# Nine tiles of 512 and eight of 256 in place of the last twenty expert tiles of 384, with casts and hand-overs moved

## The reference

```python
y = einsum('bln,mn->blm', states, C).real + x3d @ D_mat.T
x = layernorm(x + x3d + sigmoid(res_logit) * (gelu_tanh(y @ W1) @ W2))
...
probs = softmax(xf @ Wg); weights, indices = top_k(probs, 2)
for e in range(8):
    h = gelu(xf @ W1[e] + b1[e], approximate=False)     # 128 -> 512
    y = h @ W2[e] + b2[e]                               # 512 -> 128
    out = out + y * cw[:, e:e + 1]                      # weight 0 if e was not picked
x = layernorm(x + out)
```

## Time and profile before

| | us |
|---|---|
| median of 3 runs | 317.7 (317.27 to 318.15) |
| profiled execution: its own time | 319.06 |
| profiled execution: span | 317.3 |
| PE busy in the span | 275.1 (87%) |
| DVE, ACT, POOL busy | 226.2, 211.5, 211.8 |
| first `xt` (tile 0) on PE | 115.95 |
| `xt` of tile 9, begin of the last phase | 176.21 |
| last indirect DMA of POOL starts | 283.97 |

### The profile page before, as it was taken

The page is one execution under the profiler, slowest core; times in us unless marked ns, Lnnn a source line. Parts: engine busy times, 40 slices in busy tenths (PEclk is TensorE's granted clock), DMA queues, the critical chain, the costliest instruction groups (busy, mean ns, idle before and its releaser), DMA issues.

```text
span 317.3 us, 5295 instructions
## 1 busy us (share of the span) xinstructions
PE 275.1 (87%) x1303; PEld 214.6 (68%) x1303; DVE 226.2 (71%) x721; ACT 211.5 (67%) x462; POOL 211.8 (67%) x246
## 2 busy tenths in 40 slices
PE   7789996999999939859889899999999999994910
PEld 5445563756755618758777899999999999941400
DVE  2986399757997666937766688888888989701770
ACT  3653633534745544968787799999999999910580
POOL 4375795178687878607777787778778777670680
PEclk9999998799999976979999999999999999996875
DMA  5995110121221244448888765655655654317761
GB/s 90 303 331 154 34 34 0 33 75 44 84 67 44 84 167 164 156 147 290 298 295 302 259 212 171 219 209 166 229 189 186 213 192 171 116 46 293 284 173 50
DMA packets 35687, 52.18 MB, mean 164 GB/s; under 512 B 5320, under 2 KB 26320, under 8 KB 35656
## 3 DMA queue, kind: packets, MB, share of 16 engines
q1 hardware_dynamic: 29940, 41.74, 39.6%
q0 software_dynamic: 4832, 9.97, 9.5%
q10 hardware_dynamic: 884, 0.12, 0.2%
HBM read 16.99 MB, written 13.86 MB: 97 GB/s over the span
## 4 chain that ended last, share of the span: by engine, by line
PE 39%; POOL 23%; issue 13%; SPq 8%; DVE 7%; DMA 6%; ACT 1%; ACTq 0%; POOLq 0%; DVEq 0%
POOL slots_d L479 15%; PE bank L1097 10%; PE bank L1099 9%; PE bank L1098 9%; PE bank L1184 2%; POOL rstd L469 2%; SPq L364 2%; PE bank L1201 2%; DVE work L734 2%; DMA late<-slots_d 2%; PE bank L1245 2%; PE bank L1152 2%; POOL results_d L485 2%; DMA rows<-results_d 1%; POOL early L513 1%
## 5 line engine op out<-in xcount | busy, mean ns | idle before, releaser
L485 POOL DMA_INDIRECT results_d<-work,dest x87 | 92.6, 1065 | 28.0 <-issue 25.6
L479 POOL DMA_INDIRECT slots_d<-rows,slot_i x64 | 65.6, 1025 | 28.6 <-issue 18.6
L982 DVE TENSOR_TENSOR h_l<-h,h_h 128x384 fp32r<-128x384 f32 x116 | 65.0, 561 | 18.7 <-ACT h_h L636 16.0
L631 ACT ACTIVATE h<-bank,buse 128x384 f32<-128x384 f32 x116 | 67.9, 585 | 7.2 <-PE bank L1099 3.6
L1097 PE MATMUL bank<-h_h,wuse 128*128 128x384 f32 x116 | 44.8, 387 | 3.1 <-DVE h_l L982 2.7
L1097 PE MATMUL bank<-xbt_h,wuse 128*128 128x384 f32 x116 | 41.0, 353 | 1.7 <-DVE xbt_l L968 1.3
L1099 PE MATMUL bank<-xbt_h,wuse 128*128 128x384 f32 x116 | 40.0, 345 | 0.0
L1098 PE MATMUL bank<-xbt_l,wuse 128*128 128x384 f32 x116 | 40.0, 345 | 0.0
L1099 PE MATMUL bank<-h_h,wuse 128*128 128x384 f32 x116 | 39.3, 339 | 0.0
L1098 PE MATMUL bank<-h_l,wuse 128*128 128x384 f32 x116 | 39.2, 338 | 0.0
L560 ACT ACTIVATE h<-bank 128x512 f32<-128x512 f32 x32 | 18.9, 598 | 25.0 <-PE bank L1099 24.4
(11 more groups left out here) (200 smaller groups left out, 553.0 us busy)
## 6 DMA issues: line engine op xcount, KB each, us to landing
wuse<-fw SPq DMA_DIRECT2D x37, 512.0 KB, 3.5
late<-slots_d SPq DMA_DIRECT2D x29, 195.0 KB, 2.7
fw<-in_L_ffn_W_dram SPq DMA_DIRECT2D x16, 256.0 KB, 6.1
work<-in_L_attn_x3d_dram SPq DMA_DIRECT2D x8, 256.0 KB, 6.1
rows<-results_d SPq DMA_DIRECT2D x4, 512.0 KB, 5.2
work<-results_d SPq DMA_DIRECT2D x4, 512.0 KB, 9.2
out_dram<-fw SPq DMA_DIRECT2D x8, 256.0 KB, 2.3
slots_d<-zeros SPq DMA_DIRECT2D x9, 195.0 KB, 6.4
```

The lines of the kernel that those rows point to most:

```text
L479: pool.indirect_dma_start(out=slots_d, out_offset=bass.IndirectOffsetOnAxis(ap=slot_i[:, k, i:i + 1], axis=0), in_=rows[:, k, i, :], in_of ...
L485: pool.indirect_dma_start(out=results_d, out_offset=bass.IndirectOffsetOnAxis(ap=dest[:, SQ * g + q:SQ * g + q + 1], axis=0), in_=yo[:, g ...
L631: act.activation(h32[:, b % 2, 0:SLOTS], H_PS[b % 2][:, 0:SLOTS], ACT.Gelu, bias=buse[:, k, b:b + 1]).then_inc(sm["gelu_b"], 1)
L982: dve.tensor_tensor(ht_l[b], h32[:, b % 2, 0:SLOTS], ht_h[b].bitcast(F32), ALU.subtract).then_inc(sm["hbl_ready"], 1)
```

## The change

**Tiles.** Tiles 0 to 8 stay. The twenty tiles of 384 behind them become seventeen: 512, 512, then 256 and 512 in turn, and a 256 at the end (nine of 512, eight of 256). The slots of that phase fall from 7680 to 6656, the 128-row blocks of all phases (`NCOL`) from 87 to 79. Their table needs other arithmetic on DVE (`unit_counts`, `unit_origins`, `full_tables`, `odd_tables`, in the steps of tiles 2 to 4). The result ring `yo` has 60 blocks with a place written out for each tile (`home`).

**Casts.** ACT makes all 16 weight casts; POOL keeps the subtractions, with `norm(0)` behind ten of them.

**Hand-over.** First-layer weights of tiles 0 and 1 are copied by SP, all others by DVE. SP's queue between chunks and tiles is written anew; ACT's two row copies (L537) become DMAs of SP. The routing weights of the last group, the table of tiles 3 to 8 and the first-layer weights of tile 3 move on DVE to the end of tile 1. `rows_of(7)` with the last exp and two table loads moves on ACT from tiles 1 and 2 to the head of tile 1's step, and one table load ahead of `rows_of(6)`. On PE `xt(3)` moves from the end of tile 1's step into that of tile 2.

```diff
-CASTS_BY_ACT = (3, 4, 4)
+FIRST_BY_SP = 2
+CASTS_BY_ACT = (3, 8, 5)
...
+    units = (pairs[-1] - sure[-2] * SLOTS + E * (HALF - 1)) // HALF
+    fulls = (units - E) // 2
+    LAST = fulls + E
+    MT = sure[-2] + LAST
...
+    parts = [SQ] * begins[-1] + [FQ_MAX] + [FQ_MAX, HALF // P] * E
...
+            sp.wait_ge(sm["fw_lo"], NFW)
+            sp.wait_ge(sm["route_ready"], 1)
+            first_weights(0)
+            second_weights(0)
+            for g in range(2):
+                sp.wait_ge(dispatched[g], 16 * 2 * tokens_of(g)[1])
+            load(0, 0)
+            sp.wait_ge(sm["pre_a"], HB * NCH)
+            first_weights(1)
+            load(1, 1)
+            second_rows(NCH - 2)
+            second_weights(1)
+            load(2, 0)
+            second_rows(NCH - 1)
+            for n in range(1, PHASES):
+                second_weights(begins[n] - 1)
...
                 for g in range(begins[n], ends[n]):
                     load(g, g % 2)
-                    if g == 2:
-                        sp.wait_ge(sm["pre_a"], HB * NCH)
                     if g not in begins:
                         second_weights(g - 1)
-                    if g in FIRST_BY_SP:
-                        first_weights(g)
...
             for n in range(NFW):
-                if n in (7, 13):
-                    norm((7, 13).index(n))
+                if n == 10:
+                    norm(0)
                 weights_low(n)
+            norm(1)
             norm(2)
             for g in range(NG - 1):
-                at = (5, 4, 4)[g]
+                at = (4, 4, 5)[g]
...
+            def last_softmax():
+                rows_of(NCH - 1)
                 softmax_exp(NG - 1)
                 act.preload_act_table_set("gelu_and_others")
...
+            def next_tiles():
+                route_weights(NG - 1)
+                tile_tables(1)
+                dve.wait_ge(sm["route_ready"], 2)
+                held.append(expert_of(begins[1]))
+                weights1(begins[1], begins[1] % 2, held[begins[1]])
...
-            pieces = {(0, 0): first_choice, (0, 1): lambda: route_choice(NG - 1, 1), (0, 3): last_hits, (1, 1): last_slots,
-                      (2, 1): lambda: route_weights(NG - 1), (3, 1): lambda: tile_counts(PHASES - 1), (4, 1): last_tiles}
+            pieces = {(0, 0): lambda: route_choice(NG - 1, 0), (0, 1): lambda: route_choice(NG - 1, 1), (0, 2): last_exponents,
+                      (0, 3): lambda: route_hits(NG - 1), (1, 1): last_slots, (1, 3): next_tiles,
+                      (2, 1): unit_counts, (2, 3): unit_origins,
+                      (3, 1): full_tables, (4, 1): last_tiles}
```

More of the change, by code:

```diff
@@ L81, in build @@
     MMAX = max(b - a for a, b in zip(begins, ends))
-    NSL = MT * SLOTS
+    MEARLY = max(b - a for a, b in zip(begins[:-1], ends))
+    assert fulls == E + 1
+    parts = [SQ] * begins[-1] + [FQ_MAX] + [FQ_MAX, HALF // P] * E
+    col = [sum(parts[:g]) for g in range(MT + 1)]
+    NCOL = col[-1]
+    home = []
+    for g in range(MT):
+        start = home[-1] + parts[g - 1] if g else 0
+        home.append(start if start + parts[g] <= YO else 0)
+    NSL = NCOL * P
     CAP = T + SLOTS
@@ L260, in build, with group_returned, returned_all @@
         w2_loaded = [sem(f"w2_loaded{i}") for i in range(2)]
-        kept = MT - YO
-        GROUP = kept // 3
-        assert kept % 3 == 0
+        GROUP = 3
+        def group_returned(g):
+            return min(g // GROUP, 3)
+        def returned_all(eng, i):
+            a, b = GROUP * i, (GROUP * (i + 1) if i < 3 else MT)
+            eng.wait_ge(returned[i], 16 * (col[b] - col[a]))
+        freed = {}
+        for g in range(MT):
+            if home[g] < col[g]:
+                over = [n for n in range(g) if home[n] < home[g] + parts[g] and home[g] < home[n] + parts[n]]
+                assert max(over) < 3 * GROUP
+                i = group_returned(max(over))
+                if i not in freed.values():
+                    freed[g] = i
         dispatched = [sem(f"dispatched{i}") for i in range(NG)]
@@ L567, in chunk @@
                     y_high(c + 1)
-                for n in cast[2:]:
+                else:
+                    act.preload_act_table_set("gelu_and_others")
+                for n in cast[4:]:
                     weights_high(n)
@@ L914, in tile_tables @@
                 dve.tensor_scalar(first[:, a:b], rj[:, 0:M], float(ZROW), None, ALU.min).then_inc(sm["route_ready"], 1)
-                if not tail:
-                    link(dve.tensor_scalar(use, under, -1.0, float(M), ALU.mult, ALU.add))
-                    link(dve.scalar_tensor_tensor(out=use, in0=use, scalar=0.0, in1=left, op0=ALU.max, op1=ALU.min))
-                    link(dve.tensor_tensor(taken[:, n + 1, :], taken[:, n, :], use, ALU.add))
+                link(dve.tensor_scalar(use, under, -1.0, float(M), ALU.mult, ALU.add))
@@ new lines, in unit_origins @@
+            def unit_origins():
+                total, rest, unit, two_units, odd, base, upto, under, step_e, upto_odd, step_odd = (tl[:, i, :] for i in range(11))
+                link(dve.tensor_tensor(under, upto, two_units, ALU.subtract))
+                dve.tensor_tensor_scan(upto_odd, ones[:, 0:E], odd, 0.0, ALU.mult, ALU.add)
+                dve.scalar_tensor_tensor(out=origin[:, 2, 0:E], in0=two_units, scalar=float(FULL), in1=base, op0=ALU.mult, op1=ALU.add)
+                link(dve.scalar_tensor_tensor(out=origin[:, 1, 0:E], in0=under, scalar=-float(FULL), in1=base, op0=ALU.mult, op1=ALU.add))
+                dve.tensor_tensor(step_odd, origin[:, 2, 1:E + 1], origin[:, 2, 0:E], ALU.subtract)
+                link(dve.tensor_tensor(step_e, origin[:, 1, 1:E + 1], origin[:, 1, 0:E], ALU.subtract))
@@ L990, in step @@
                             meta(g + 1, 1 - k)
-                        if b == 3 and far and g + 2 not in FIRST_BY_SP:
+                        if b == 3 and far and g + 2 != begins[1]:
                             weights1(g + 2, k, held[g + 2])
```

239 lines of the change are left out of this document (129 added, 110 removed).

## The result

The changed kernel takes 306.29 us in the median (304.98 to 306.68, 4 runs) against 317.83 of the kernel before in the same comparison (4 runs): a ratio of 0.9632, 95% interval 0.9598 to 0.9665, or 11.5 us less. The forecast was 305.5. A second comparison on a chip where the kernel before took 319.54 gave 307.13 and 0.9608 (0.9566 to 0.9649).

The account below looks back on a forecast made before the run. PE was taken to bound the last phase, with ACT near. Gains of 5.0 us up to xt(9) and 11.4 in the last phase, less 4.2 of hand-overs, make -12.2: 317.7 to 305.5 us, range 298 to 313 (8 in 10).

Parts of the forecast that it names:

- First stage, -6.05: Chunk 2's routing: with casts off POOL, its subtractions end earlier and no longer stretch DVE; 17.94 to 11.89, 6.05 us less.
- rival 3: Chunk 2's stall stays, through POOL's subtractions or ACT's casts delaying the first chunks; 6.05 lost, 311.6 us; chance 0.10.
- xt(3) at 137.3: Start of tile 3 on PE, against 139.06 before: its load waits for the late table, leaving 1.8 of 6.05 us.
- the 22.0: From xt(0) at 109.9 to DVE's start on the work put at tile 1's end, at 131.9: 22.0 us.
- xt(9) at 171.2: Start of tile 9 on PE: six tiles at SP's queue pace take 33.9 us; 5.0 us earlier than 176.21.
- the queue's 5.64 a tile: Tiles 3 to 8: SP's queue period of 6.85 us less 1.21 for first-layer weights, which DVE now copies.
- Last phase, -11.4 + 4.2: Tiles from 9 on: wide and narrow tiles save PE 11.4 us; ACT and hand-overs cost back 4.2.
- hold-back of 0.6 a pair: Last phase: PE held by ACT's narrow steps and tighter hand-overs, 0.6 us for each of seven pairs, +4.2.
- ACT's price: Last phase: each ACT instruction costs 0.146 us beside 0.875 ns per column, so a narrow step takes ACT 4.45 us.
- rival 5: Last phase: narrower ACT instructions cost 0.3 us each, a pair 12.7 us; no gain, 321.8 us; chance 0.04.
- rival 4: Last phase: PE's granted clock falls from 2.4 to 1.2 GHz; 329 us if a third runs low; chance 0.06.
- The end behind them stays: After the last tile but one: POOL's last six sends begin there as before, and the time behind them is unchanged.

## Why the prediction was right

The time lies 0.8 us from the forecast. The steps hold in their sizes, and all but one in their mechanism: the pace of tiles 3 to 8 was not the one named. That the sum came so close is in part luck, as several terms are off and cancel.

- **First stage, -6.05.** Chunk 2 lost 5.54; the 6.47 at tile 0 hold 0.94 more, from a shorter wait for its rows, that the step did not count. The cause was the one named, and rival 3's form of it (subtractions alone suffice) is true as a mechanism but did not strike, as they end at 43.6 (42.4 foretold), ahead of the routing. What the step missed is that part of the 17.94 was a low granted clock behind the wait. It varies, and with it the worth of the step: 3 to 4 us by the times of the run with casts on POOL, 5.5 by the profiled executions before and after.
- **xt(3) at 137.3.** 138.00. The two table loads cost 2.60 (2.56 foretold), the routing weights and the table at the end of tile 1 2.16 (2.2). The latter start 23.1 us behind xt(0) and not 22.0; which term of the 22.0 is short was not measured (PE's mean granted clock from xt(0) to xt(3) is 0.71, before it was 0.80). Moving the table shows that it, and no dispatch, held tile 3.
- **xt(9) at 171.2.** 170.63. Taking the weights off SP's queue is worth 4.3 us, as the run with them put back shows. But the pace that is left is not the queue's 5.64 a tile. The tiles take 4.62 to 7.00, the longer ones wait for DVE, in part behind the new table, and behind tile 3 only xt(9) waits for rows (0.57). The prediction had DVE's load as a sum over six tiles, 31.5, just under the queue's 33.9; that the measured 32.6 lies between them is luck for the mechanism named.
- **Last phase, -11.4 + 4.2.** From xt(9) to the first of the last six sends 94.01, against 94.3 (101.5 - 11.4 + 4.2). Wide tiles take 6.47, not 6.42. The hold-back of 0.6 a pair was 0.68 in all, but its parts were otherwise: 0.39 is what a narrow tile takes even among narrow ones, with ACT nearly full, 0.24 the hand-over between widths, the rest the wide tile.
- **ACT's price.** Among narrow ones a narrow tile at 3.70 with ten ACT instructions and 2304 columns is (3.70 - 2.02)/10 = 0.17 each beside the 0.875 ns per column, near the 0.146 taken from the step of 384; rival 5 (0.3 each) falls.
- **Clock.** 1.00 in the last phase; rival 4 did not come about.
- **The end.** "The end behind them stays" was right for this order, since 4 + 2 sends equal 3 + 3: the last send starts 5.55 us behind PE's last back transpose and did so 5.22 before. It hid that the order itself was worth more than the hold-back that I weighed.

Open is why the medians with the earlier table differ by more than the traces do; single executions of one kernel scatter by 1 to 4 us here, and the low clock behind waits is one source that the traces show.

## What to carry to other kernels

Where tiles of two sizes share a phase, put the order to the test: what stands last sets the serial tail behind the bound engine, and here that was worth more than the waits between sizes. When a wait goes, ask whether the bound engine also ran slow behind it, and count that part as uncertain. Where a chain of engines makes a wait, moving its first user moves the wait, as two runs here show; what would shorten the chain was not tried.

## What the runs showed of the hardware that was not expected

POOL can be the slowed one as well as DVE. Its subtraction takes 1.27 us where DVE does nothing (34.74 in the kernel before), and the same beside the small instructions of chunk 2, where DVE is the one held up (6.17 us for five). Beside DVE's 128x512 instructions on `work` it takes up to 2.2, and 1594 ns in the mean with all sixteen early, 1411 before. And one wait of 2.9 us of PE was followed by 7 to 8 us at a mean granted clock of 0.63 or 0.76, in two executions whose instructions up to it were alike.
